# Gated linear attention on Trainium2: the loop written out, the group preparation half a beat earlier, both gates in one product, one PSUM bank of two per batch

## The chip, the core and the metric

The kernel runs on one core of one Trainium2 chip. It is one launch that computes a whole decoder of two layers in nine phases, one after the other. The metric is the device time of the launch in microseconds; of several runs the median counts. The change touches one phase, gated linear attention ("gla"), which takes some 580 us of the launch.

## The reference, cut to what matters

x is 64 batches of 128 tokens by 128 channels, in float32. The phase computes `x = layernorm(x + _L1_attn_ref(x, ...))` with 16 heads (H) of 8 channels (d):

```python
Q = (X @ q1_w.T).reshape(b, l, H, d)
K = (X @ k1_w.T).reshape(b, l, H, d)
V = X.reshape(b, l, H, d)
W = K[..., :, None] * V[..., None, :]
G = jax.nn.sigmoid(X.reshape(b, l, H, d) @ gw_w.T)
G = jnp.clip(G, 1e-06, None)
Gc = jnp.exp(jnp.clip(jnp.cumsum(jnp.log(G), axis=1), -30.0, 30.0)) + 1e-06
R = jax.nn.silu(K @ sw_w.T)[..., None]
Wc = jnp.cumsum(W * R / Gc[..., None], axis=1) * Gc[..., None]
O1 = jnp.einsum('blhd,blhde->blhe', Q, Wc)
E = V[:, 1:] - O1[:, :-1]
...
W2 = jnp.cumsum(K2[..., :, None] * E[..., None, :], axis=1)
O2 = jnp.einsum('blhd,blhde->blhe', Qm, W2)
out = (O1.reshape(b, l, dim) + O2.reshape(b, l, dim)) @ c_proj_w.T
```

Two gates come from the same rows: G from X and R from K = X @ k1_w.T. Qm is a leaky rectifier of the queries, K2 a sigmoid of a third projection.

## The kernel before, in words

Each cumulative sum is written as masked attention: scores of keys against queries, a triangular mask, a product with the values. A batch goes through three stages: s1 (four score products into the four banks `sc`, mask, into `a1`, then v1, sixteen products of 32 columns that give O1 in bank `o1b`), e (E = V minus shifted O1, two products, copied to `ep`), s2 (four score products into the same four banks, mask, into `a2`), v2 (O2 in bank `o2b`) and out (two products with `wo`). Of the four score banks VectorE masks two directly from PSUM (L2265 for s1, L2293 for s2). ScalarE copies the other two to SBUF (L2183, L2192), and GpSimd masks them there (L2332, L2342).

The work is pipelined over batches by hand. A **step** is a group of four batches, a **beat** (p = 0 to 3) one batch. In a beat TensorE does, in this order: s1 of batch n, e of batch n-2 (L2083, L2084), out of batch n-3 (L2089, L2090), a first half of the next group's preparation (`head(..., (p, 0))`), s2 of batch n-1, the second half (`(p, 1)`), v1 of n-1 and v2 of n-2 (L2063). ScalarE reads O1 and O2 out (L2200, L2206) at the end of its beat. The engines run their own instruction streams in order and meet at semaphores; there is no other scheduler.

The preparation of a group (`head`), per engine in order: GpSimd copies X to `xc`; TensorE transposes it (L2022) and ScalarE reads it as `xT`; the keys (L2028, read as `kT`); both gates, eight small products, four from `xT` with `gw` and four from `kT` with `sw` (L2032, L2033); VectorE takes them as `ga` and `gr` (L2224, L2225), ScalarE applies Exp, Ln, Exp (L2147 to L2151), VectorE finishes them (L2231, L2233); K2 (L2035, `k2a` on VectorE L2227, three ScalarE activations L2154 to L2158); the queries (L2038, `qT`, `qs`, L2235 `qmT`); the cumulative gate (L2041, clip L2239, Exp, L2242, reciprocal, L2246 `rg8`); both gates spread by transposition (L2046, L2051); and the products `kf` (L2250) and four `qg` (L2254), which the next group's s1 needs. ScalarE also writes four `qn` (L2172), which s2 needs. VectorE further does, once per group, the statistics of the four finished rows in beat 2 (L117, L121) and the normalisation in beat 3 (`normalise`, four instructions, L134); GpSimd computes the inverse deviation in between (L126, L128).

The first step, the last two steps and the first preparation stand outside the hardware loop; the 14 steps between run in a loop of two steps per turn (`run`, L1972 to L1980). What a batch needs first is asked for by the wait that names all of the group's VectorE instructions:

```python
if b == 0:
    pe.wait_ge(by_dve, (g + 1) * N_DVE)
```

## Time and profile before

| | us |
|---|---|
| runs shown, median of 3 | 3989.52 |
| lowest and highest | 3985.66, 3991.07 |
| profiled execution, device time | 3961.34 |
| its span | 3959.3 |
| the phase's first to last TensorE product | 2630.5 to 3194.7 |

In the profiled execution TensorE is busy 87% of the span, VectorE 64%, ScalarE and GpSimd 50% each; the granted clock of TensorE is 0.925 of full speed. In the profile a line number names the instruction's place in the code, `XC<-gla_scores` its output and input. An idle time in brackets is the time the engine stood still just before, with the instruction whose semaphore came last.

### The profile page before, as it was taken

Reading aid. Unit: us, or ns where it says so; the run is one execution under the profiler, and the core shown is the slowest. Engines: PE = TensorE matmul, PEld = TensorE weight load, DVE = VectorE, ACT = ScalarE, POOL = GpSimd, SP = SyncE. Lnnn points to the kernel's source line nnn. Section 1 sums busy time; section 2 is a strip of 40 time slices with the busy share of each in tenths; the row PEclk is TensorE's granted clock in tenths of the full one; section 3 lists DMA queues with packets and bytes.
Section 4 is the critical chain, followed back from the end, with each engine's and each line's share of the span. In section 5 each row is a group of like instructions: output and inputs, shape, how many; then the busy total and the mean of one; then the engine's idle time right before and its main releaser. Section 6 shows DMA issues by size and latency. Waiting matters only on the chain. (4 is left out here: it accounts for less than half of the span.)

```text
span 3959.3 us, 104241 instructions
## 1 busy us (share of the span) xinstructions
PE 3444.1 (87%) x41696; PEld 2239.8 (57%) x41696; DVE 2546.9 (64%) x5780; ACT 1967.4 (50%) x3810; POOL 1998.7 (50%) x1726
## 2 busy tenths in 40 slices
PE   7888988988599999886999998868888879999676
PEld 3444444544355555564666666645555557777676
DVE  6878878878477677475556647666666645554365
ACT  5555555554255555442665653335555536664254
POOL 5767667666377777654111115436666621111555
PEclk8999999999799999997999999979999979998598
DMA  3212121211920000000000000000000000000386
GB/s 123 76 71 78 69 80 70 77 72 62 297 65 2 2 2 2 16 1 17 5 5 5 5 3 10 5 6 2 2 2 2 2 11 6 7 6 12 99 266 197
DMA packets 48993, 182.11 MB, mean 46 GB/s; under 512 B 11679, under 2 KB 23074, under 8 KB 39361
## 3 DMA queue, kind: packets, MB, share of 16 engines
q1 hardware_dynamic: 44224, 167.68, 12.7%
q0 software_dynamic: 4352, 8.47, 0.6%
q8 instruction: 312, 5.11, 0.5%
q14 instruction: 105, 0.85, 0.1%
HBM read 167.13 MB, written 43.65 MB: 53 GB/s over the span
## 5 line engine op out<-in xcount | busy, mean ns | idle before, releaser
L494 DVE TENSOR_TENSOR_SCAN XC<-ssm_dA,ssm_db 128x2048 f32<-128x2048 f32 x128 | 565.6, 4419 | 145.0 <-PE ssm_db L349 122.0
L556 POOL TENSOR_TENSOR XC<-XC,XB 128x1536 f32<-128x1536 f32 x128 | 492.9, 3851 | 293.1 <-DVE XC L494 180.5
L363 PE MATMUL ssm_y<-XC,ssm_wt 128*128 128x512 f32 x1024 | 493.3, 626 | 1.6 <-POOL XC L556 1.6
L1130 POOL TENSOR_TENSOR self_pm<-self_pT,self_wt 128x512 f32<-128x512 f32 x256 | 321.9, 1292 | 175.6 <-ACT self_pT L904 175.6
L438 ACT ACTIVATE ssm_dA<-ssm_delta,ssm_nega 128x508 f32<-128x508 f32 x512 | 324.9, 707 | 106.2 <-DVE XC L494 106.2
L363 PEld LDWEIGHTS ssm_y<-XC,ssm_wt 128*128 128x128 f32 x1024 | 196.0, 199 | 228.7 <-issue 219.3
L1136 POOL TENSOR_TENSOR XC<-XC,XB 128x128 f32<-128x128 f32 x128 | 58.7, 459 | 402.3 <-DVE XB L1038 402.3
L2332 POOL TENSOR_TENSOR XC<-XC,gla_wt 128x512 f32<-128x512 f32 x128 | 160.6, 1275 | 157.7 <-ACT XC L2183 157.7
L349 PE MATMUL ssm_db<-XB,ssm_dxT 32*128 32x128 f32 x4096 | 174.6, 299 | 71.9 <-DVE XC L494 70.3
L349 PEld LDWEIGHTS ssm_db<-XB,ssm_dxT 32*128 32x128 f32 x4096 | 145.6, 198 | 136.7 <-DVE XC L494 113.0
L1457 DVE TENSOR_REDUCE narrow_nmax<-narrow_scores 128x4 f32<-128x308 f32 x256 | 105.1, 472 | 156.4 <-PE narrow_scores L1274 156.3
L904 ACT ACTIVATE self_pT<-self_scores 128x512 f32<-128x512 f32 x256 | 132.2, 602 | 137.2 <-PE self_scores L814 137.2
L126 POOL TENSOR_SCALAR narrow_rstd<-narrow_mv 128x4 f32<-128x4 f32 x16 | 3.6, 228 | 379.6 <-DVE narrow_mv L121 379.6
L1024 DVE TENSOR_REDUCE self_nmax<-self_scores 128x4 f32<-128x512 f32 x256 | 158.6, 680 | 46.8 <-PE self_scores L788 46.8
L2342 POOL TENSOR_TENSOR XC<-XC,gla_wt 128x512 f32<-128x512 f32 x128 | 160.9, 1278 | 42.9 <-ACT XC L2192 42.6
L1606 PEld LDWEIGHTS mlp_yp<-mlp_wt,mlp_h 128*128 128x128 f32 x1024 | 133.2, 192 | 58.1 <-issue 56.4
L904 ACT ACTIVATE cross_pT<-cross_scores 77x512 f32<-77x512 f32 x256 | 131.0, 591 | 69.8 <-PE cross_scores L814 69.6
L1382 ACT ACTIVATE narrow_pT<-narrow_scores 77x512 f32<-77x512 f32 x256 | 131.0, 591 | 68.4 <-PE narrow_scores L1300 68.4
L2265 DVE TENSOR_TENSOR XC<-gla_scores,gla_wt 128x512 f32<-128x512 f32 x128 | 82.4, 685 | 100.3 <-PE gla_scores L2057 100.3
L1634 ACT ACTIVATE mlp_h<-mlp_hp,mlp_bias 128x512 f32<-128x512 f32 x128 | 88.0, 687 | 109.0 <-PE mlp_hp L1598 109.0
L1024 DVE TENSOR_REDUCE cross_nmax<-cross_scores 128x4 f32<-128x308 f32 x256 | 104.0, 467 | 57.8 <-PE cross_scores L788 57.8
L1598 PE MATMUL mlp_hp<-mlp_zT,mlp_wt 128*128 128x512 f32 x256 | 134.3, 611 | 1.5 <-ACT mlp_zT L1628 1.5
(430 smaller groups left out, 8690.4 us busy)
## 6 DMA issues: line engine op xcount, KB each, us to landing
XB<-c_rows SPq DMA_DIRECT2D x64, 1024.0 KB, 4.7
experts_we<-in_w_experts SPq DMA_DIRECT2D x72, 579.0 KB, 4.6
sorted<-in_padding SPq DMA_DIRECT2D x1, 33280.0 KB, 112.2
experts_rt<-sorted SPq DMA_DIRECT2D x72, 65.0 KB
ssm_xT<-in_xT SPq DMA_DIRECT2D x16, 256.0 KB, 4.6
self_wt<-in_w_self SPq DMA_DIRECT2D x1, 1412.0 KB, 6.5
mlp_wt<-in_w_mlp SPq DMA_DIRECT2D x1, 1347.0 KB, 5.7
cross_ctx_t<-in_ctx SPq DMA_DIRECT2D x16, 77.0 KB
```

The lines of the kernel that those rows point to most:

```text
L349: mm = pe.matmul(of_batch(db, b)[:, :, 32 * c:32 * c + 32], dxT[rows, slot, half, c, :], diag(slot, c)[rows, nq, :].rearrange("p (k t) -> ...
L363: mm = pe.matmul(yp[half][:, :].rearrange("p (b t) -> p b t", b=GROUP), ident, of_state(states(32, at), k), start=False, stop=(nq == 3 and ...
L438: o = act.activation(dA[:, p % 2, :].rearrange("p (b k t) -> p b k t", b=GROUP, k=4)[:, :, k, 1:T], by_batch(delta[:, slot, half, :])[:, : ...
L494: dve.tensor_tensor_scan(states(0, p).rearrange("p m t -> p (m t)"), dA[:, p % 2, :], db[:, :], 0.0, ALU.mult, ALU.add).then_inc(h_ready, 1)
L556: pool.tensor_tensor(states(32, p).rearrange("p (b k) t -> p b k t", k=4)[:, :, 0:3, :], states(0, p).rearrange("p (b k) t -> p b k t", k= ...
L904: act.activation(pT[0:TK, n % 2, r, :], sc[r][0:TK, :], ACT.Exp).then_inc(exp_ready, 1)
L1024: dve.tensor_reduce(nmax[:, r, :], sc[r][:, 0:4 * TK].rearrange("p (h t) -> p h t", h=4), AX.X, ALU.max, negate=True).then_inc(max_ready, 1)
L1130: pool.tensor_tensor(pm[:, n % 2, r, :].rearrange("p (h t) -> p h t", h=4), pT[:, n % 2, r, :].rearrange("p (h t) -> p h t", h=4), bcast(V ...
L1598: pe.matmul(hp[j][:, :], w2[:, j * P:(j + 1) * P], zT[:, g % 2, :]).then_inc(h_mm, 1)
L1606: mm = pe.matmul(yp[g % 2][:, b * C:(b + 1) * C], h[:, g % 2, j, b * T:(b + 1) * T], w3[:, j * C:(j + 1) * C], start=(j == 0), stop=(j == 3))
L2332: pool.tensor_tensor(a1(b, r), a1(b, r), bcast(tri, 1, 4), ALU.mult).then_inc(m1_pool, 1)
L2342: pool.tensor_tensor(a2(b, r), a2(b, r), bcast(tri0, 1, 4), ALU.mult).then_inc(m2_pool, 1)
```

## The change

It does five things, all in this phase.

1. The hardware loop is gone: 17 steps are written out, with constant semaphore values and addresses.
2. The preparation is moved: transposes and `xT` in (0,0), keys and `kT` in (0,1), gates in (1,0), K2 and the gates' finish in (1,1), cumulative gate and queries in (2,0), `rg8`'s transposes, `kf` and `qmT` in (2,1), `gc8`'s transposes and the four `qg` in (3,0). On ScalarE the four `qn` move behind the read-outs of O1 and O2 in beats 2 and 3. On VectorE the normalisation moves from ahead of the read-out of `out` in beat 3 to the end of that beat.
3. Both gates are one product of `xT`: `gs` holds `gw` and `wkT @ sw` side by side (made once at the start), so four products of 32 columns take the place of eight of 16.
4. O1, e, out and O2 of a batch share one bank, `acc[b % 2]`, 128 columns each, in place of `o1b` and `o2b`. v1 of a batch waits for the read-out of the batch two before it (`out_read`); its waits for `o1_ready` and `e_ready`, and v2's for `out_read`, are gone.
5. GpSimd's copy of X to `xc` is gone: the transposes and `vp` read X.

```diff
-            step(0, 0, True)
-            with eng.Fori(1, NG - 2, 2) as g:
-                step(g, 1, True)
-                step(g + 1, 0, True)
-            step(NG - 1, 1, False)
-            step(NG, 0, False)
+            for g in range(NG + 1):
+                step(g, g % 2, g + 1 < NG)
...
+            pe.matmul(pj[1][:, 0:H], wkT, sw).then_inc(fold_mm, 1)
...
+                if half == (1, 0):
                     pe.wait_ge(by_act, g * N_ACT + 2)
                     for b in range(GROUP):
-                        pe.matmul(pj[1][:, b * H:(b + 1) * H], xT[:, b * T:(b + 1) * T], gw)
-                        mm = pe.matmul(pj[1][:, BH + b * H:BH + (b + 1) * H], kT[:, b * T:(b + 1) * T], sw)
+                        mm = pe.matmul(pj[1][:, b * 2 * H:(b + 1) * 2 * H], xT[:, b * T:(b + 1) * T], gs[:, :])
                     mm.then_inc(proj_mm, 1)
+                if half == (1, 1):
                     pe.matmul(pj[0][:, :], wk2, xT[:, :]).then_inc(proj_mm, 1)
                 if half == (2, 0):
-                    pe.wait_ge(by_dve, g * N_DVE + 3)
+                    pe.wait_ge(by_dve, g * N_DVE + 5)
+                    pe.matmul(pj[1][:, 2 * BH:3 * BH], tri, ga[:, 0, :]).then_inc(proj_mm, 1)
                     pe.matmul(pj[0][:, :], wq, xT[:, :]).then_inc(proj_mm, 1)
                 if half == (2, 1):
-                    pe.wait_ge(by_dve, g * N_DVE + 4)
-                    pe.matmul(pj[1][:, 2 * BH:3 * BH], tri, ga[:, 0, :]).then_inc(proj_mm, 1)
-                if half == (3, 0):
-                    pe.wait_ge(by_act, g * N_ACT + 10)
-                    pe.wait_ge(by_dve, g * N_DVE + 10)
+                    pe.wait_ge(by_act, g * N_ACT + 11)
+                    pe.wait_ge(by_dve, g * N_DVE + 9)
                     for b in range(GROUP):
                         mm = pe.matmul(pj[0][:, b * T:(b + 1) * T], rg8[:, b * P:(b + 1) * P], ident)
                     mm.then_inc(proj_mm, 1)
...
-                        if needed(n):
-                            pe.wait_ge(o1_ready, n)
                         if needed(n - 1):
-                            pe.wait_ge(e_ready, n - 1)
-                        if lagged(g, p, 2, slot):
-                            pe.wait_ge(e_ready, n)
-                        values(o1b, vp[:, s, b], a1, b, av1_mm)
+                            pe.wait_ge(out_read, n - 1)
+                        values(vp[:, s, b], a1, b, 0, av1_mm)
...
+            def shifted_queries(g, slot, p):
+                if p >= 2:
+                    act.wait_ge(by_dve, g * N_DVE + 11)
+                    for j in {2: (0, 1), 3: (2, 3)}[p]:
                         act.activation(by_batch(qn[:, slot, j, :])[:, :, 1:T], by_batch(qmT[:, :])[:, :, 0:T - 1],
                                        ACT.Identity, scale=own_head[:, j:j + 1]).then_inc(by_act, 1)
...
                 if half == (1, 1):
+                    dve.wait_ge(by_act, g * N_ACT + 5)
+                    dve.tensor_scalar(ga[:, 0, :], ga[:, 0, :], -1.0, float(np.log(1e-6)), ALU.mult, ALU.max)\
+                        .then_inc(by_dve, 1)
+                    dve.tensor_tensor(gr[:, 1, :], gr[:, 1, :], ga[:, 1, :], ALU.mult).then_inc(by_dve, 1)
                     dve.wait_ge(proj_mm, g * PJ + 4)
                     dve.tensor_scalar(k2a[:, :], pj[0][:, :], -0.02 / float(np.sqrt(C)), BIG, ALU.mult, ALU.min)\
                         .then_inc(by_dve, 1)
```

VectorE, beats 1 and 2 of a step, before. L2265 masks s1, L2293 masks s2; the gates' finish is L2231 and L2233.

```order
L2293 TENSOR_TENSOR XC<-gla_scores,gla_wt 128x512 x2
L2222 ISA
L2224 TENSOR_SCALAR gla_ga<-gla_proj 128x128
L2225 COPY gla_gr<-gla_proj 128x128
L2226 REGISTER_ALU
L2227 TENSOR_SCALAR gla_k2a<-gla_proj 128x512
L2261 REGISTER_ALU
L2265 TENSOR_TENSOR XC<-gla_scores,gla_wt 128x512 x2
L2272 COPY gla_ep<-gla_first 128x16x8
```

And in the change, from the first look at the gates to the next beat's mask of s1. L2295 masks s2, L2270 masks s1.

```order
L2229 TENSOR_SCALAR gla_ga<-gla_proj 128x128
L2230 COPY gla_gr<-gla_proj 128x128
L2295 TENSOR_TENSOR XC<-gla_scores,gla_wt 128x512 x2
L2233 TENSOR_SCALAR gla_ga<-gla_ga 128x64
L2235 TENSOR_TENSOR gla_gr<-gla_gr,gla_ga 128x64
L2237 TENSOR_SCALAR gla_k2a<-gla_proj 128x512
L2270 TENSOR_TENSOR XC<-gla_scores,gla_wt 128x512 x2
```

The gates' finish, which stood in beat 2 behind the statistics, now stands in beat 1 directly behind the mask of s2, and `k2a` stands behind it.

ScalarE, beats 1 and 2, before. L2192 copies s2's scores for GpSimd, L2200 and L2206 read out O1 and O2.

```order
L2192 ACTIVATE XC<-gla_scores 128x512 x2
L2146 ISA
L2147 ACTIVATE gla_ga<-gla_ga 128x128
L2148 ISA
L2149 ACTIVATE gla_ga<-gla_ga 128x128
L2150 REGISTER_ALU
L2151 ACTIVATE gla_ga<-gla_ga 128x64
L2200 ACTIVATE gla_o1T<-gla_first 128x128
L2206 ACTIVATE gla_o2T<-gla_second 128x128
```

And in the change. L2186 copies s2's scores, L2194 and L2200 read out O1 and O2.

```order
L2139 ACTIVATE gla_ga<-gla_ga 128x128
L2141 ACTIVATE gla_ga<-gla_ga 128x128
L2143 ACTIVATE gla_ga<-gla_ga 128x64
L2186 ACTIVATE XC<-gla_scores 128x512 x2
L2146 ACTIVATE gla_k2a<-gla_k2a 128x512
L2148 ACTIVATE gla_k2a<-gla_k2a 128x512
L2150 ACTIVATE gla_k2T<-gla_k2a 128x512
L2194 ACTIVATE gla_o1T<-gla_out 128x128
L2200 ACTIVATE gla_o2T<-gla_out 128x128
```

The gates' three functions now stand ahead of s2's copy, and the three of K2, which followed in beat 2, now stand between that copy and the read-out of O1.

## Rows read from the trace of the kernel before

**Rows 1.** Timeline of TensorE: start us, busy us, line, operation, [idle before, releaser]; s1 at a step's start
```profile
2753.11 1.14 PE L2057 MATMUL gla_scores<-gla_qg,gla_kf 32*128 32x512 f32 x8 [3.02 <-DVE gla_qg L2254]
...
3162.23 1.14 PE L2057 MATMUL gla_scores<-gla_qg,gla_kf 32*128 32x512 f32 x8 [2.53 <-DVE gla_qg L2254]
```

**Rows 2.** Waits, 2670 to 3140 us: waiter, releaser, us in all, times, longest
```profile
PE gla_scores L2057 <- DVE gla_qg L2254: 38.6, 14, 3.2
...
PE gla_first L2083 <- ACT gla_o1T L2200: 9.2, 14, 0.7
...
PE gla_scores L2057 <- DVE XC L2293: 4.6, 14, 1.1
...
PE gla_proj L2041 <- DVE gla_ga L2231: 4.4, 13, 0.3
```

**Rows 3.** Timeline of TensorE in one group
```profile
2800.13 0.38 PE L2033 MATMUL gla_proj<-gla_wt,gla_kT 128*128 128x16 f32 x2
2800.36 1.10 PE L2035 MATMUL gla_proj<-gla_xT,gla_wt 128*128 128x512 f32 x2
...
2803.28 1.14 PE L2057 MATMUL gla_scores<-gla_qg,gla_kf 32*128 32x512 f32 x8
2804.35 0.49 PE L2083 MATMUL gla_first<-gla_neg,gla_o1T 128*128 128x128 f32 x2
...
2805.34 1.02 PE L2038 MATMUL gla_proj<-gla_xT,gla_wt 128*128 128x512 f32 x2
...
2807.77 0.43 PE L2041 MATMUL gla_proj<-gla_ga,gla_wt 128*128 128x64 f32 x2 [0.34 <-DVE gla_ga L2231]
...
2821.59 1.14 PE L2057 MATMUL gla_scores<-gla_qg,gla_kf 32*128 32x512 f32 x8 [3.20 <-DVE gla_qg L2254]
```

**Rows 4.** Windows: from:to, us, busy (count) of PE, PEld, DVE, ACT, POOL, granted clock, DMA
```profile
2822.90:2826.30 3.40, 3.40 (x16) 1.92 (x15) 1.76 (x4) 1.06 (x2) 2.49 (x2) 0.51 0.02 5
3162.20:3166.20 4.00, 3.65 (x36) 1.94 (x40) 1.90 (x5) 1.30 (x3) 2.09 (x2) 1.00 0.00 0
```

**Rows 5.** Timeline, 2668 to 2670 us: GpSimd's masks beside VectorE's gate operations
```profile
2668.07 1.09 ACT L2183 ACTIVATE XC<-gla_scores 128x512 f32<-128x512 f32 x2 [0.79 <-PE gla_scores L2057]
2668.75 2.51 POOL L2332 TENSOR_TENSOR XC<-XC,gla_wt 128x512 f32<-128x512 f32 x2 [1.86 <-ACT XC L2183]
...
2669.48 0.60 DVE L2231 TENSOR_SCALAR gla_ga<-gla_ga 128x64 f32<-128x64 f32 x1
...
2670.00 1.35 DVE L2233 TENSOR_TENSOR gla_gr<-gla_gr,gla_ga 128x64 f32<-128x64 f32 x1
```

**Rows 6.** Source line 2242: ns min/median/max, first and last start; then the tail's normalisation
```profile
L2242 DVE TENSOR_SCALAR gla_gc<-gla_gc x16: 195/929/944, 2645.8 to 3152.1; 128x64 f32<-128x64 f32 x16
...
3181.47 4.00 DVE L134 TENSOR_SCALAR X<-gla_y,gla_mv,gla_rstd 128x128 f32<-128x128 f32 x4
```

**Rows 7.** Timeline of VectorE in the same group
```profile
2800.75 0.28 DVE L2225 COPY gla_gr<-gla_proj 128x128 f32<-128x128 f32 x1
...
2804.49 1.29 DVE L2265 TENSOR_TENSOR XC<-gla_scores,gla_wt 128x512 f32<-128x512 f32 x2 [2.29 <-PE gla_scores L2057]
...
2806.20 0.88 DVE L117 BATCH_NORM_STATS2 gla_stats<-gla_y 128x6 f32<-128x128 f32 x4
2807.24 0.38 DVE L121 BATCH_NORM_AGGREGATE gla_mv<-gla_stats 128x2 f32<-128x6 f32 x4 [0.16 <-DVE gla_stats L117]
...
2810.23 0.22 DVE L2239 TENSOR_SCALAR gla_gc<-gla_proj 128x64 f32<-128x64 f32 x1
...
2812.33 0.69 DVE L2246 TENSOR_TENSOR gla_rg<-gla_rg,gla_gr 128x512 f32<-128x512 f32 x1
...
2818.16 2.71 DVE L2254 SCALAR_TENSOR_TENSOR gla_qg<-gla_qT,gla_wt,gla_proj 128x512 f32<-128x512 f32 x4
```

**Rows 8.** Timeline of ScalarE in the same group
```profile
2801.75 0.26 ACT L2151 ACTIVATE gla_ga<-gla_ga 128x64 f32<-128x64 f32 x1
...
2805.46 0.63 ACT L2154 ACTIVATE gla_k2a<-gla_k2a 128x512 f32<-128x512 f32 x1
```

More of the change, by code:

```diff
@@ L1957, in linear_attention_phase @@
         sc = [ph.bank(f"scores{r}") for r in range(4)]
-        o1b = ph.bank("first")
-        o2b = ph.bank("second")
+        acc = [ph.bank(f"out{i}") for i in range(2)]
         pj = [ph.bank(f"proj{i}") for i in range(2)]
-        (loaded, power_set, setup, zeroed, xc_ready, vp_ready, proj_mm, by_act, by_dve, s1_mm, s2_mm, m1_dve, m1_act,
+        (loaded, power_set, setup, zeroed, fold_mm, folded, vp_ready, proj_mm, by_act, by_dve, s1_mm, s2_mm, m1_dve, m1_act,
          m1_pool, m2_dve, m2_act, m2_pool, av1_mm, o1_ready, e_mm, e_ready, av2_mm, o2_ready, out_mm, out_read, vec,
          pool_step, x_out) = (ph.sem(n) for n in (
-             "loaded", "power_set", "setup", "zeroed", "xc_ready", "vp_ready", "proj_mm", "by_act", "by_dve", "s1_mm",
+             "loaded", "power_set", "setup", "zeroed", "fold_mm", "folded", "vp_ready", "proj_mm", "by_act", "by_dve", "s1_mm",
              "s2_mm", "m1_dve", "m1_act", "m1_pool", "m2_dve", "m2_act", "m2_pool", "av1_mm", "o1_ready", "e_mm",
@@ L1989, in closing @@
         def closing(g):
-            return not (isinstance(g, int) and g < 1)
+            return g >= 1
         def a1(b, r):
@@ L2024, in head @@
-                if half == (1, 0):
+                if half == (0, 0):
+                    if g:
+                        pe.wait_ge(by_dve, (g - 1) * N_DVE + 10)
+                    for b in range(GROUP):
+                        mm = pe.transpose(pj[0][:, b * T:(b + 1) * T], X[:, g * GROUP + b, :], ident)
+                    mm.then_inc(proj_mm, 1)
+                if half == (0, 1):
                     pe.wait_ge(by_act, g * N_ACT + 1)
-                    if needed(g):
+                    pe.wait_ge(folded, 2)
+                    if g:
@@ L2082, in step @@
                         pe.wait_ge(o1_ready, n + 1)
-                        pe.matmul(o1b[:, T:T + C], o1T[:, b % 2, :], neg[:, :], start=True, stop=False)
-                        pe.matmul(o1b[:, T:T + C].rearrange("p (r j d) -> p r j d", r=4, j=4), up, spread(vp[:, s, b]),
+                        e = acc[b % 2][:, T:T + C]
+                        pe.matmul(e, o1T[:, b % 2, :], neg[:, :], start=True, stop=False)
+                        pe.matmul(e.rearrange("p (r j d) -> p r j d", r=4, j=4), up, spread(vp[:, s, b]),
                                   start=False, stop=True).then_inc(e_mm, 1)
@@ L2124, in step @@
                         pe.wait_ge(m2_pool, 2 * (n + 1))
-                        if needed(n):
-                            pe.wait_ge(out_read, n)
-                        values(o2b, ep[:, b % 2], a2, b, av2_mm)
-            run(pe, head, step)
+                        values(ep[:, b % 2], a2, b, 3 * T, av2_mm)
+            run(head, step)
         @block.scalar
@@ L2205, in step @@
                             act.wait_ge(out_mm, n)
-                        act.activation(o2T[:, :], o2b[:, 0:T], ACT.Identity).then_inc(o2_ready, 1)
-            run(act, head, step)
+                        act.activation(o2T[:, :], acc[b % 2][:, 3 * T:4 * T], ACT.Identity).then_inc(o2_ready, 1)
+                    if more:
+                        shifted_queries(g + 1, 1 - slot, p)
+            for half in HALVES:
+                head(0, 0, half)
+            for p in range(GROUP):
+                shifted_queries(0, 0, p)
+            for g in range(NG + 1):
+                step(g, g % 2, g + 1 < NG)
         @block.vector
@@ L2296, in step @@
                         head(g + 1, 1 - slot, (p, 1))
-            run(dve, head, step)
+                    if p == 3 and closing(g):
+                        dve.wait_ge(pool_step, g * 2)
+                        normalise(dve, lambda b: X[:, (g - 1) * GROUP + b, :], lambda b: y[:, 1 - slot, b, :],
+                                  mv[:, :, :], rstd[:, :]).then_inc(x_out, 1)
+            run(head, step)
         @block.gpsimd
@@ L2343, in step @@
                                                ALU.mult).then_inc(m2_pool, 1)
-            run(pool, head, step)
+            run(head, step)
 def experts_phase(nc, env, name, wd, w, out):
```

120 lines of the change are left out of this document (50 added, 70 removed).

## The prediction

> **What bounds the kernel now.** I read the timeline of TensorE first. Two starts of s1 at a step's start lie 409.12 us and twelve steps apart [rows 1], so a step of four batches takes 34.09 us. The chain of waits then says where TensorE stands still in 14 steps: 38.6 us behind the four `qg`, 9.2 behind the read-out of O1, 4.6 behind the masks of s2, 4.4 behind the gates [rows 2]. That is 56.8, or 4.06 us a step, and 2.76 of it is one stop: s1 of a new group waits for the last `qg`. A second loss follows it. After the stop TensorE runs 3.4 us at a granted clock of 0.51, its 1.2 GHz level, though it is busy throughout [rows 4], which costs half of that, 1.7 us. The other stops of 2.7 us and more are followed by such a fall too; the one of 2.53 us [rows 1] is followed by a full clock [rows 4]. So a step is 34.09 = 4.06 idle + 1.7 slow + 28.3 of products at full clock. TensorE is the bound, broken by VectorE's chain.
>
> The reader should also see what VectorE's small operations cost. In rows 5, GpSimd's two masks run from 2668.75 to 2671.26; VectorE's finish of the first gate, 64 columns, takes 0.60 us, until GpSimd's first mask is over, and that of the second takes 1.35 us, until the second is over. The addition to `gc` takes 195 ns with GpSimd idle and 929 ns as a rule [rows 6]. And the last normalisation, four small instructions, takes 4.00 us [rows 6]. An SBUF-to-SBUF instruction of VectorE waits for the GpSimd instruction that runs, and gets one chance between two of them. The Trainium skill (SBUF — State Buffer, "Who interferes with whom") has this as an exclusive lock on a shared port pair, in which the order of issue decides who blocks; the rows above agree.
>
> **Part by part, gates first.** A gate product's place is 0.23 us (2800.13 to 2800.36) [rows 3]; four of eight go, so 0.9 us a step. The keys' part is folded into the weights once, for one product and two copies: nothing. The copy of X on GpSimd was off the path, and so is its absence. The banks: v1 now waits for the sum `y` of the same beat, which VectorE does right after its masks and `ep`, while TensorE has e, out, half a preparation and s2 to do: nothing, and that is some 3 us of cover. The loop: its turn shows no stop of its own in the waits; I take nothing.
>
> **The stop on `qg` goes.** The spread of `gc8` moves a half ahead, the four `qg` stand before the mask of s2 in beat 3, and the normalisation behind it. What is late next is that mask. Count from s1 of beat 3: s1 and e, out end at 1.07 + 0.99 = 2.06 [rows 3]. Four `gc8` products, as long as e and out with their loads, end near 3.2. Four `qg` take 2.7 [rows 7], to 6.0, and the mask 1.29 [rows 7], to 7.3. TensorE has s2 (1.07) and v1 and v2 (1.9) after the `gc8` products and is done at 6.1. **Stop C: 1.2 us**, in place of 2.76.
>
> **The order of beat 1 decides the rest.** Count from the end of the gate products. VectorE takes its second copy 0.39 later, ScalarE its third function 1.00 after that [rows 3, 7, 8], s2's copy some 0.2 later, and GpSimd's first mask 0.68 after that copy starts [rows 5]: 2.26. VectorE must mask s2 first: s2 1.07, hand-over 0.14, masks 1.20 to the next instruction: 2.41, and only then comes the gates' finish. So GpSimd starts first, by 0.15 us. The finish of the first gate then waits for one mask of 1.25, that of the second for the next, and is done at 2.26 + 2.5 + 0.1 = 4.86 instead of about 2.6. `k2a` follows until 5.5. Beat 2 starts at 1.07 + 2.92 (K2, v1, v2, 2800.36 to 2803.28) = 3.99. So `k2a` ends 1.5 into beat 2. ScalarE's three functions of K2, 0.63 each [rows 8], end at 3.4, and **only behind them** comes the read-out of O1, which e waits for, 0.3 more: 3.7. TensorE has been free since 1.07. **Stop A: 2.6 us**, where rows 2 have 0.66.
>
> **Beat 2.** e and out end at 4.65, the sum `y` at 5.3. The statistics take 1.33 (2806.20 to past 2807.53) [rows 7], then the chain from clip to `rg8`, 2810.23 to 2813.02 = 2.79 [rows 7]. In it `gc`'s addition now meets GpSimd only in its small operations, so 0.74 less: 2.05. That is 8.7. Meanwhile TensorE does tri (0.4), queries (1.0) and s2 (1.07), ready at 7.05, and in the new order waits for `rg8` there. **Stop B: 1.7 us.** The old waits of 0.34 for the gates, 0.33 for the masks of s2 and 0.66 for O1 go.
>
> **The sum.** A step was 34.09. Out go 4.06 idle, 1.7 slow, 0.9 gates; in come A + B + C = 5.5, less 0.2, as these count from the end of issue and rows 2 from the end of work: 5.3. That is 32.7 us. Its price is between 0 (all under B) and 1.7 (all outside); I take 0.5, nearer to the cover. Step: 33.2, or 0.9 less. Over 15 steps: 13.5 us. The **first preparation** is a bare chain at the low clock: four gate products less at twice 0.23 is 1.8; GpSimd's copy ahead of the transposes, between 0 and a mask's 1.25, say 0.6; the gate's Exp no more behind two activations like those of rows 8, 1.2; in all 4 (bounds 2 and 5). In the **tail** the sum `y` stood behind the 4.00 us of rows 6 and v2 behind it: 2 (bounds 0 and 3). Together 19.5 us: the profiled execution's 3961.3 would become 3941.8. That execution is 28.2 below the median of the runs; on the median it is 3989.5 - 19.5 = **3970 us**.
>
> **A rule against it and one for it.** The Trainium skill (TensorE: Matmul & The Clock Gate, "Why this matters for your kernels") names a length of gap below which the clock keeps up, and 2.6 lies below it; by it the falls would be gone and the result 7 us lower. Its section on oscillation there tells of a kernel that fell once for each short tile, which is the first rival.
>
> **Rivals.**
> 1. *Every fall at full price.* For: stops A, B and C make three chances a step, and a fall that begins late lies on v1 and v2, with no slack. Against: B's slack follows A directly. Step 32.7 + 1.7 = 34.4; 15 x 0.3 = 4.5 lost, 6 won at the ends: 3988. Chance 0.17.
> 2. *VectorE wins the race of beat 1.* The margin is 0.15 us in 2.3. Then the gates finish at 2.6, `k2a` ends ahead of beat 2, O1 is read at 1.7 into it, A shrinks to 0.6; `rg8` comes earlier too, at 7.5, but s2 ends at 5.2, so B is 2.3; C is 1.1 and M1 behind the normalisation adds 0.3. Idle 4.3, step 31.7 without falls, 32.6 with them in half of the steps: 15 x 1.5 to 2.4 and 6: 28 to 42 lower, 3954 in the middle. Chance 0.23.
> 3. *Slower: the normalisation meets GpSimd.* It now runs behind the mask of s2 in beat 3, beside GpSimd's masks of the same scores. I expect one wait, as its last mask is just ending. If GpSimd lags by more than one mask, each of the four waits, 4.00 us as in rows 6, and the next s1's mask, due 1.3 us after the normalisation's free run, comes some 2.4 late, s2 with it. It decides from the point where GpSimd's next pair starts before the second of the four. Step 33.2 + 2.4 = 35.6: 15 x 1.5 = 23 lost, 6 won: 4007. Chance 0.1.
> 4. *The written-out streams stall on code*, or the change does not do what it says: no row of this phase shows it, the phases around it are written out and TensorE runs full there. Chance 0.05, for either sign.
>
> My forecast has 0.45.
>
> **How the numbers follow.** About 0.2%, 8 us, is what a measurement of this kernel can tell from no change. Faster takes the forecast (0.45), rival 2 (0.23) and a little of the fourth: 0.7. Same is rival 1: 0.18. Slower is rival 3 and the rest: 0.12. The forecast's own range is 3960 to 3982 (fall 0 to 1.2 a step, ends 2 to 8). The range leaves out the far half of rival 2 and rival 3: 3946 to 3994.
>
> **What would show it.** In the profile after: no wait of s1 on `qg`; a wait of e (the product with `neg`) on the read-out of O1 of about 2.6 us once a step; a wait of the `rg` transposes on `rg8` of about 1.7; s1 on the mask of s2 about 1.2; the second gate's product on VectorE near 1.3 us instead of 0.21, and `gc`'s addition near 0.2; four gate products a step. Steps of 33.2 us. It is wrong if the second gate stays at 0.21 (rival 2), if the normalisation takes 4 us (rival 3), or if TensorE stands still for another reason than these three.

## The result, and the profile after

| | before | after |
|---|---|---|
| median (lowest to highest), us | 3989.35 (3979.49 to 3991.07), 5 runs | 3952.53 (3938.21 to 3967.42), 5 runs |
| ratio to before, 95% interval | | 0.9917 [0.9898, 0.9935] |
| profiled execution: time, span | 3961.34, 3959.3 | 3938.21, 3936.4 |
| gla, in the profiled execution | 582.1 | 541.8 |
| narrow attention, the phase behind it | 434.7 | 428.6 |
| experts, the last phase | 324.2 | 346.8 |

The change is faster by 36.8 us on the medians; the interval of the ratio means 26 to 41 us. The forecast was 19.5 us. The profiled execution of the kernel before is none of its five runs and lies 18 us below their lowest. Phases are measured between the starts of the weight transfers that open them.

The first thing to see is that the phase that was edited gained 40.3 us, while the profiled pair differs by 23.1. The rest lies in phases that the change does not touch: narrow attention is 6.1 us shorter, and the experts are 22.6 us longer. The experts show ScalarE standing still without a releaser, six times, once for 13.70 us. Timeline of ScalarE, then the waits of 3580 to 3940 us, after:

```profile
3685.60 0.21 ACT L2540 ACTIVATE experts_alpha<-experts_best 128x4 f32<-128x4 f32 x1 [13.70 <-issue]
```
```profile
ACT experts_alpha L2540 <- issue: 27.6, 6, 13.7
```

The same kernel run again on another chip had 325.1 us there, and so had every experiment, within 2 us. So the change does not bring it. Whether it belongs to this one execution or to the chip of this measurement stays open: on that chip the medians of both kernels, 3989 and 3953 us, lie 27 and 22 us above those of the same kernels in the experiments, 3962 and 3930. A reader who had compared the two spans alone would have halved the gain of the edit.

**TensorE's waits after**, 2670 to 3120 us (waiter, releaser, us in all, times, longest), beside [rows 2]:

```profile
PE gla_out L2081 <- ACT gla_o1T L2194: 24.4, 14, 2.4
PE gla_proj L2043 <- DVE gla_rg L2248: 22.2, 14, 1.7
PE gla_scores L2054 <- issue: 15.4, 14, 1.1
```

The 38.6 us on `qg` are gone, and the waits on the masks and the gates too. What is left are the three stops that the prediction called A (e on the read-out of O1), B (`rg8`'s transposes) and C (s1 behind the mask of s2). On the timeline of TensorE they look like this:

```profile
2727.30 0.49 PE L2081 MATMUL gla_out<-gla_neg,gla_o1T 128*128 128x128 f32 x2 [2.40 <-ACT gla_o1T L2194]
...
2732.31 1.13 PE L2043 MATMUL gla_proj<-gla_wt,gla_rg 128*128 128x128 f32 x8 [1.69 <-DVE gla_rg L2248]
...
2758.43 0.49 PE L2081 MATMUL gla_out<-gla_neg,gla_o1T 128*128 128x128 f32 x2 [1.26 <-ACT gla_o1T L2194]
...
2763.43 1.59 PE L2043 MATMUL gla_proj<-gla_wt,gla_rg 128*128 128x128 f32 x8 [1.69 <-DVE gla_rg L2248]
2764.95 1.94 PE L2060 MATMUL gla_out<-XC,gla_vp 128*32 128x128 f32 x32
...
2775.16 1.14 PE L2054 MATMUL gla_scores<-gla_qg,gla_kf 32*128 32x512 f32 x8 [1.11 <-issue]
```

Stop A has two lengths, 2.40 us in six steps (one of them 2.38) and 1.26 in eight. Stop C names no releaser, but VectorE's timeline does: the mask of s2 (two instructions, 1.28 us from 2773.78) ends as s1 starts, and the normalisation behind it runs free, four instructions in 1.31 us:

```profile
2773.78 1.28 DVE L2295 TENSOR_TENSOR XC<-gla_scores,gla_wt 128x512 f32<-128x512 f32 x2
2774.97 1.31 DVE L134 TENSOR_SCALAR X<-gla_y,gla_mv,gla_rstd 128x128 f32<-128x128 f32 x4
```

Added up, the idle time did not fall. It is (24.4 + 22.2 + 15.4) / 14 = 4.43 us a step, against 4.06 before. What fell is the time at the low clock, and the work between the stops. Windows of TensorE after (from:to, us, busy (count) of PE, PEld, DVE, ACT, POOL, granted clock): behind a stop of 2.40 us the clock stays full in five of six steps; the falls lie at 2764, 2825 and 2893, and there are no others.

```profile
2728.30:2731.30 3.00, 2.32 (x14) 0.73 (x12) 2.31 (x13) 1.03 (x4) 2.92 (x4) 1.00 0.00 0
2764.00:2767.40 3.40, 3.40 (x53) 3.00 (x56) 1.77 (x3) 0.48 (x2) 1.79 (x2) 0.51 0.02 5
2825.50:2828.90 3.40, 3.40 (x14) 1.45 (x13) 2.50 (x14) 1.24 (x4) 3.19 (x4) 0.52 0.01 2
```

In the kernel before, 13 of the same fourteen steps had a fall, the first of them 6.8 us long. Only the step that began behind a stop of 1.27 us had none.

**Where a step's time went.** Over the fourteen steps behind the first, a step took 34.11 us before and 31.85 after, 2.26 less. Windows over these steps, before and then after, and of single steps in two of the experiments below. In `e4` (the kernel before, written out) they are a step with a fall and one without, in `e6` (the change with eight gate products) one without:

```profile
2684.70:3162.23 477.53, 418.39 (x5545) 266.55 (x5545) 314.13 (x714) 256.86 (x560) 313.53 (x279) 0.95 0.01 2
2679.05:3124.97 445.92, 383.79 (x5433) 245.97 (x5433) 321.47 (x711) 255.77 (x561) 307.19 (x267) 0.99 0.01 2
```
```profile
2811.74:2845.44 33.70, 29.90 (x396) 19.30 (x396) 22.45 (x51) 18.37 (x40) 22.43 (x20) 0.95 0.01 2
2879.15:2911.68 32.53, 28.42 (x397) 18.29 (x397) 22.35 (x51) 18.38 (x40) 22.45 (x20) 1.00 0.01 2
```
```profile
2818.06:2850.05 31.99, 27.94 (x397) 18.22 (x397) 22.58 (x52) 18.24 (x41) 21.99 (x20) 1.00 0.01 2
```

With the short gaps that the waits leave out, TensorE's idle time rose from 4.22 to 4.44 us a step, and its busy time fell by 2.47, from 29.89 to 27.41. Of this, 1.1 us are the falls: one makes a step's products 1.5 us longer before (29.90 against 28.42) and 1.6 after, in fourteen steps fourteen times (the long one counted twice) against three. The gate products are 0.9. The last 0.5 us are products that take less time in the new order: `e4` and `e6` both have eight gate products and no loop, and they have 28.42 and 27.94 us of work in a step at full clock. The hardware loop has no part in it, as its cost lies in the idle time (see `e4`). Outside these steps, the first step gained 2.1 us, its start 4.4 (3.5 of it behind the first product), and the tail 2.2: there v1 waits 0.84 us for the sum `y`, where v2 waited 2.26 before.

**The race of beat 1.** VectorE's two operations that finish the gates meet GpSimd's two masks of s2. Source lines, ns min/median/max:

```profile
L2233 DVE TENSOR_SCALAR gla_ga<-gla_ga x16: 195/1060/1067, 2639.0 to 3104.7; 128x64 f32<-128x64 f32 x16
```
```profile
L2235 DVE TENSOR_TENSOR gla_gr<-gla_gr,gla_ga x16: 211/213/1343, 2639.1 to 3105.7; 128x64 f32<-128x64 f32 x16
```
```profile
L2244 DVE TENSOR_SCALAR gla_gc<-gla_gc x16: 195/195/339, 2642.2 to 3113.2; 128x64 f32<-128x64 f32 x16
```

The first waits as forecast, 1.06 us, and `gc`'s addition is free at 0.195 where it took 0.929 [rows 6]. The second has two outcomes. First a step with A = 2.40, then one with A = 1.26, timelines of GpSimd and VectorE:

```profile
2721.89 2.53 POOL L2340 TENSOR_TENSOR XC<-XC,gla_wt 128x512 f32<-128x512 f32 x2 [0.73 <-ACT XC L2186]
```
```profile
2723.15 1.34 DVE L2235 TENSOR_TENSOR gla_gr<-gla_gr,gla_ga 128x64 f32<-128x64 f32 x1
```
```profile
2754.15 2.61 POOL L2340 TENSOR_TENSOR XC<-XC,gla_wt 128x512 f32<-128x512 f32 x2 [0.72 <-ACT XC L2186]
```
```profile
2754.43 1.06 DVE L2233 TENSOR_SCALAR gla_ga<-gla_ga 128x64 f32<-128x64 f32 x1
2755.41 0.21 DVE L2235 TENSOR_TENSOR gla_gr<-gla_gr,gla_ga 128x64 f32<-128x64 f32 x1
```

In the first, VectorE gets one operation in between the two masks and stands behind the second mask with the other, until 2724.4. In the second it gets both in, and GpSimd's pair takes 0.08 us longer. The 1.13 us saved pass straight through `k2a`, K2's three functions and the read-out of O1: A is 1.14 us shorter, and so is the step (31.12 against 32.26 us).

### The profile page after: what moved, and what is told of

The parts are those of the page before. It is cut to its first block and busy times, and to the rows that moved or that the text cites. A ratio compares the mean times of both kernels' runs of the same rounds, so it can differ in the third digit from the quotient of the medians.

```text
span 3936.4 us, 102778 instructions
## 1 busy us (share of the span) xinstructions
PE 3398.2 (86%) x41570; PEld 2210.2 (56%) x41570; DVE 2549.1 (65%) x5782; ACT 1967.2 (50%) x3810; POOL 1991.1 (51%) x1710
## 5 line engine op out<-in xcount | busy, mean ns | idle before, releaser
L2270 DVE TENSOR_TENSOR XC<-gla_scores,gla_wt 128x512 f32<-128x512 f32 x128 | 82.4, 686 | 80.5 <-PE gla_scores L2054 79.4
```

## The experiments

Each ratio is to the kernel before on the same chip. There its medians were 3962.94 us (runs `e1` to `e4`), 3961.95 (`e5` to `e8`) and 3960.49 (`e9`, `e10`); times of one chip are compared with each other. The first three runs attack stop A, the largest.

### e1: the read-out of O1 ahead of K2's functions

```diff
                 if half == (1, 1):
-                    act.wait_ge(by_dve, g * N_DVE + 5)
-                    act.activation(k2a[:, :], k2a[:, :], ACT.Exp).then_inc(by_act, 1)
...
                         act.activation(o2T[:, :], acc[b % 2][:, 3 * T:4 * T], ACT.Identity).then_inc(o2_ready, 1)
                     if more:
+                        third_keys(g + 1, 1 - slot, p)
```

`third_keys` holds the wait and the three functions, and runs in beat 1.

> The changed kernel with one thing moved on ScalarE: K2's three functions stand behind the read-outs of O1 and O2 in beat 1, not ahead of them. Theory (ScalarE's order makes stop A: e waits for O1, which is queued behind K2's functions, which wait for VectorE behind GpSimd's masks): the waits of 2.40 and 1.26 us of e on the read-out of O1 are gone; the copies of s1 come later instead, up to 1 us is given back before s2; steps of 31.1 and 32.3 us become 30.2, some 24 us less than the change in the phase. Rival (the chain from the sum y to rg8 carries beat 2 whatever O1 does): stop B grows by what A loses, steps stay within 0.3 us of 31.1, and the time stays.

Measured: 3907.37 us, ratio 0.9865 [0.9844, 0.9885]; phase 530.2, steps of 30.77 but for one of 32.38 with a fall and one of 30.54. Waits of TensorE, same stretch:

```profile
PE gla_proj L2043 <- DVE gla_rg L2254: 23.2, 15, 2.3
PE gla_scores L2054 <- issue: 16.6, 15, 1.1
PE gla_scores L2054 <- ACT XC L2180: 14.4, 13, 1.1
```

Stop A is gone. It was the order on ScalarE, then, and not the computation of O1. Of A's 1.26 to 2.40 us, 1.1 came back as a wait of s2 for ScalarE's copy of scores, which now queues behind K2's functions. The step is still 0.35 us shorter than the change's short one and 1.5 shorter than its long one, and all falls but one are gone.

### e2: the gates' finish ahead of the mask of s2

```diff
-                if half == (1, 1):
                     dve.wait_ge(by_act, g * N_ACT + 5)
                     dve.tensor_scalar(ga[:, 0, :], ga[:, 0, :], -1.0, float(np.log(1e-6)), ALU.mult, ALU.max)\
                         .then_inc(by_dve, 1)
                     dve.tensor_tensor(gr[:, 1, :], gr[:, 1, :], ga[:, 1, :], ALU.mult).then_inc(by_dve, 1)
+                if half == (1, 1):
                     dve.wait_ge(proj_mm, g * PJ + 4)
```

The two operations fall to half (1, 0), which VectorE does ahead of its mask of s2.

> The changed kernel with the gates' finish on VectorE ahead of the mask of s2 in beat 1, so that it runs before GpSimd's masks of the same scores begin. Theory (the finish waits for the GpSimd instruction that runs, then for the next): the finish of the first gate falls from 1.06 us to 0.2, that of the second from 1.34 or 0.21 to 0.21 in every step, e's wait for O1 to 0.6 us, steps to 30.5 to 31.1 us, and steps of 32.3 are gone: 10 to 20 us less than the change. Rival (the small instructions are slow by themselves, or wait for ScalarE): they stay near 1 us and the time stays or rises by 5 us, since the mask of s2 is now behind a wait for ScalarE.

Measured: 3910.13 us, ratio 0.9865 [0.9845, 0.9885]; phase 528.0, steps of 30.64 but for one of 32.24 with a fall. The two operations take 0.196 and 0.219 us in every step: ahead of the mask there is no GpSimd to meet. Waits:

```profile
PE gla_proj L2043 <- DVE gla_rg L2248: 24.5, 15, 1.7
PE gla_scores L2054 <- issue: 16.6, 15, 1.1
PE gla_out L2081 <- ACT gla_o1T L2194: 11.8, 15, 0.9
```

So the race, taken out, is worth as much as the last link of the chain to O1: A is 0.8 us here, in every step. `e1` and `e2` are 56 and 53 us below before, where the change run again (`e5`) is 31.5 below.

### e3: both

The edits of `e1` and `e2` together.

> Both moves of the two runs before. Theory: no stop A, stop B 1.8 us, stop C 1.1 us, steps of 30.1 us, no fall of the clock between the first step and the last; 25 to 30 us less than the change. Rival (beat 2 is carried by VectorE's chain): no better than the better of the two alone.

Measured: 3915.07 us, ratio 0.9884 [0.9864, 0.9904]; phase 531.1.

```profile
PE gla_proj L2043 <- DVE gla_rg L2254: 33.8, 15, 2.3
PE gla_scores L2054 <- issue: 16.6, 15, 1.1
```

Together they are no better than either. Part of that is the clock: the profiled execution had three falls, one of 6.8 us, in steps of 31.88, 33.45 and 32.14 us, and the other eleven steps took 30.54. That alone is 0.1 to 0.2 us less than in `e1` and `e2`, and the waits say why it is no more. No wait on O1 is left, but the wait on `rg8` has grown from 1.6 to 2.3 us. TensorE and VectorE in one beat 2, which starts with s1 at 2789.75:

```profile
2796.58 1.13 PE L2043 MATMUL gla_proj<-gla_wt,gla_rg 128*128 128x128 f32 x8 [2.31 <-DVE gla_rg L2254]
```
```profile
2792.36 0.28 DVE L2289 TENSOR_TENSOR gla_y<-gla_out,X 128x128 f32<-128x128 f32 x1
2792.68 0.87 DVE L117 BATCH_NORM_STATS2 gla_stats<-gla_y 128x6 f32<-128x128 f32 x4
2793.70 0.38 DVE L121 BATCH_NORM_AGGREGATE gla_mv<-gla_stats 128x2 f32<-128x6 f32 x4
...
2794.51 0.62 DVE L2250 TENSOR_SCALAR gla_gc<-gla_gc 128x64 f32<-128x64 f32 x1 [0.32 <-ACT gla_gc L2146]
```

The same places measured in four kernels, in us. The first column counts from the start of s1 of beat 2 to the sum `y`, the second is the addition to `gc`, the third counts from `y` to the transposes of `rg8`, the last from s1 to them:

| | s1 to `y` | addition | `y` to transposes | s1 to transposes |
|---|---|---|---|---|
| `e2` | 3.12 | 0.20 | 3.81 | 6.93 |
| `e3` | 2.61 | 0.62 | 4.22 | 6.83 |
| `e8` (below) | 3.11 | 1.28 | 3.49 | 6.60 |
| `e10` (below) | 2.61 | 0.73 | 3.39 | 6.00 |

TensorE has e 0.8 us earlier in `e3`, and the sum `y` comes 0.5 earlier, as VectorE is busy with its mask of s1 until then. Of these 0.5 the addition takes 0.42 back: it now starts while GpSimd still has its mask. So 0.1 us is left, and the step shows it (30.54 against 30.64). The chain to `rg8` sets the end, and 1.3 us of it are the statistics. Runs `e8` and `e10` go on from there.

### e4: the kernel before, written out

```diff
-            with eng.Fori(1, NG - 2, 2) as g:
-                step(g, 1, True)
-                step(g + 1, 0, True)
+            for g in range(NG + 1):
+                step(g, g % 2, g + 1 < NG)
```

> The kernel before with the loop written out and nothing else. Theory (the loop's registers and turn cost little): 2 us less in the phase, 0.25 us for each second step, with all the stops and falls of before; 0 to 5 us less in all. Rival (the written-out code is what brings or takes time): more than 10 us less in the phase, or stalls without a releaser in this or the later phases and 10 us or more above before.

Measured: 3954.47 us, ratio 0.9982 [0.9972, 0.9991], 4 to 11 us; phase 570.5 against 582.1. Most steps are 33.7 us instead of 34.1, and four are 32.53. Both are more than was expected: the phase is 11.6 us shorter in the profiled execution, and 10.2 of it lie in the fourteen steps.

```profile
PE gla_scores L2053 <- DVE gla_qg L2250: 34.0, 14, 2.5
PE gla_first L2079 <- ACT gla_o1T L2196: 9.2, 14, 0.7
```

The stop on `qg` is 2.4 us a step instead of 2.76, the other waits are as before. VectorE is not what became faster: in both kernels its last `qg` ends 10.5 us behind the start of s1 of beat 3. But TensorE starts the next s1 0.25 us after that end between the two steps of a turn and 0.5 to 0.7 us after it where a turn ends (at 2821.59 0.72 us: the `qg` of [rows 7] end at 2820.87), and 0.05 us after it in `e4`. The loop thus cost 0.3 to 0.4 us a step on TensorE's own side, and it showed as part of the wait on `qg`. The four short steps are those without a fall, and one of them began behind a short stop of 1.07 us. Of the 13 stops of 2.53 us, three had no fall behind them, while before each stop of 2.73 us and more had one.

### e5 and e6: the change again, and with eight gate products

`e5` is the change as it stands. The edit of `e6`:

```diff
-                        mm = pe.matmul(pj[1][:, b * 2 * H:(b + 1) * 2 * H], xT[:, b * T:(b + 1) * T], gs[:, :])
+                        pe.matmul(pj[1][:, b * 2 * H:b * 2 * H + H], xT[:, b * T:(b + 1) * T], gw)
+                        mm = pe.matmul(pj[1][:, b * 2 * H + H:(b + 1) * 2 * H], kT[:, b * T:(b + 1) * T], sw)
```

> The changed kernel once more, unaltered. Its first profile lost 22.6 us in the last phase (experts, 346.8 us against 324.2 before), in which nothing is changed, in stops of up to 13.7 us without a releaser. Theory (these belong to single executions or places, not to the change): the experts phase takes 324 to 326 us as in the three kernels derived from it, gla 541 to 545 us, and the kernel stands 40 to 47 us below the one before. Rival (the change brings them): experts again near 347 us and some 25 to 33 us below.

> The changed kernel with the gates as eight products of 16 columns again (the folded weights are made but not used). Theory (four products more are 0.9 us a step on TensorE, on the path): steps 0.9 us longer, the first preparation 1.8 us, 15 us in the phase. Rival (the later gates are hidden, as beat 1 has no stop of TensorE): a change within 3 us, or the race between VectorE's finish and GpSimd's first mask comes out another way and steps differ by 1.1 us either way.

Measured: `e5` 3930.45 us, ratio 0.9912 [0.9893, 0.993], phase 550.8, experts 325.1; `e6` 3943.56, ratio 0.9943 [0.9929, 0.9957], phase 565.1. Steps without a fall are 31.12 in the one and 32.0 in the other: 0.9 us, the four places of 0.23 us in [rows 3], and 13.1 us on the time. The waits are alike (rg 18.6 and 18.0, O1 27.2 and 26.2 us), so it is work and not a stop that goes. Of the expectation for `e5`, the experts came true; its phase and its distance from the kernel before did not, and the falls are the larger part of why.

`e5` also shows the same program with eight falls in the fourteen steps, where the other execution had three, with steps of up to 33.85 us and a phase 9 us longer. The stops are the same (2.4 or 1.25, 1.69, 1.1), with the long A in seven steps. The falls cost 10.0 us over the fourteen steps, against 3.4; `e6` and `e9` had eight as well. On TensorE's timeline a fall is seen in the durations: e takes 0.80 us instead of 0.49, the transposes 1.83 instead of 1.13. The window shows that the fall at 2764 was a long one:

```profile
2764.52 0.80 PE L2081 MATMUL gla_out<-gla_neg,gla_o1T 128*128 128x128 f32 x2 [2.39 <-ACT gla_o1T L2194]
...
2931.03 1.83 PE L2043 MATMUL gla_proj<-gla_wt,gla_rg 128*128 128x128 f32 x8 [1.69 <-DVE gla_rg L2248]
```
```profile
2764.00:2770.80 6.80, 6.28 (x21) 3.27 (x21) 3.38 (x14) 2.95 (x8) 3.77 (x4) 0.50 0.00 1
```

The fall at 2764 began in the last half microsecond of A and lasted 6.8 us, twice as long as the others; stop B is gone in that step, and still it is 33.50 us, 1.24 longer than one without a fall. A fall of 3.4 us behind the same stop, at 2733, cost nothing, and one at 2798 cost 0.8. The one at 2931 began behind B and cost 1.6.

### e7: the normalisation back ahead of the read-out of `out`

```diff
+                    if p == 3 and closing(g):
+                        dve.wait_ge(pool_step, g * 2)
+                        normalise(dve, lambda b: X[:, (g - 1) * GROUP + b, :], lambda b: y[:, 1 - slot, b, :],
+                                  mv[:, :, :], rstd[:, :]).then_inc(x_out, 1)
...
                         dve.tensor_tensor(y[:, s, b, :], acc[b % 2][:, 2 * T:2 * T + C], X[:, n, :], ALU.add).then_inc(out_read, 1)
...
-                    if p == 3 and closing(g):
-                        dve.wait_ge(pool_step, g * 2)
-                        normalise(dve, lambda b: X[:, (g - 1) * GROUP + b, :], lambda b: y[:, 1 - slot, b, :],
```

> The changed kernel with the normalisation back where it was, ahead of the read-out of out in beat 3 on VectorE. Theory (VectorE's chain in beat 3 sets stop C: the sum y, the qg and the mask of s2 all come 1.4 to 2 us later, and v1, which now waits for the sum, too): stop C grows from 1.1 to 2.4 to 3 us, steps by 1.3 to 1.9 us, 20 to 28 us in the phase, with more falls of the clock. Rival (no difference, as the normalisation must be done anyway before the next mask): within 3 us.

Measured: 3993.00 us, ratio 1.0067 [1.0052, 1.0082]; phase 609.2, 58 us longer than `e5`. One move turns the change from 31.5 us faster into 31 slower. VectorE, GpSimd and TensorE in one beat 3:

```profile
2900.06 3.67 DVE L134 TENSOR_SCALAR X<-gla_y,gla_mv,gla_rstd 128x128 f32<-128x128 f32 x4
2903.65 0.28 DVE L2287 TENSOR_TENSOR gla_y<-gla_out,X 128x128 f32<-128x128 f32 x1
```
```profile
2899.65 2.49 POOL L2330 TENSOR_TENSOR XC<-XC,gla_wt 128x512 f32<-128x512 f32 x2 [4.38 <-ACT XC L2177]
```
```profile
2904.07 1.08 PE L2060 MATMUL gla_out<-XC,gla_vp 128*32 128x128 f32 x32 [2.43 <-DVE gla_y L2287]
```

Four small instructions meet GpSimd's masks of s1 and take 3.67 us where they take 1.31 behind the mask of s2. The sum `y` waits behind them, and v1 waits for `y` because O1 and out share a bank now. A step without a fall is 34.34 us against 31.12: 2.43 are this wait of v1, and 0.7 a longer stop C, where the expectation had put the growth. Over fourteen steps that is 45 of the 58 us. There were 15 falls in them, against eight in `e5`. This is the mechanism of rival 3, at a place which the change avoids. It also tells what parts 2 and 4 of the change owe each other: by the waits in the code, the shared bank is free of cost only because the normalisation was moved away. The move back with two banks was not run.

### e8: the statistics in beat 0 of the next step, on top of e2

```diff
-        y = ph.sb("y", [P, 2, GROUP, C])
+        y = ph.sb("y", [P, 3, GROUP, C])
...
-                    if p == 2 and closing(g):
-                        dve.wait_ge(out_read, g * GROUP)
-                        row_stats(dve, lambda b: y[:, 1 - slot, b, :], stats[:, :, :], mv[:, :, :], vec, (g - 1) * VEC, mark)
...
+                    if p == 0 and g >= 2:
+                        rows_of(g - 2)
+                    if p == 3 and g >= 2:
+                        norm_of(g - 2)
```

`rows_of` does the statistics of a group, at the end of beat 0; `norm_of` normalises it, a step later than before, and GpSimd's inverse deviation moves with it.

> The kernel with the early gate finish, and with the statistics of a group's rows moved out of beat 2 to the end of beat 0 of the next step (three slots of y, normalisation one step later). Theory (stop B is y, statistics, clip, Exp, addition, reciprocal, rg8, with 1.33 us of it the statistics): rg8 comes 1.3 us earlier if nothing else holds it, or 0.6 us if the addition or rg8 now meets GpSimd's masks, which it did not before; stop B from 1.6 to 0.3 or 1.0 us, steps of 29.4 to 30.1 us against 30.64, 8 to 19 us less than with the early finish alone. Rival (another chain takes over): steps of 30.6 us again.

Measured: 3900.96 us, ratio 0.9842 [0.9828, 0.9855]; all fourteen steps 30.31 to 30.33 us, no fall. The wait on `rg8` fell only from 1.6 to 1.3 us (20.1 us in 15), though 1.3 us of statistics left the path to it. The source line of the addition shows where the rest went:

```profile
L2244 DVE TENSOR_SCALAR gla_gc<-gla_gc x16: 195/1286/1298, 2643.1 to 3093.0; 128x64 f32<-128x64 f32 x16
```

Starting earlier, the chain runs into GpSimd's masks of s1, which it used to miss: 1.29 us instead of 0.20, 1.1 of the 1.3 given back. It is the wait of beat 1 again, met by a chain that had become faster.

### e9: two banks again

```diff
-        acc = [ph.bank(f"out{i}") for i in range(2)]
+        o1b = ph.bank("first")
+        o2b = ph.bank("second")
...
+                            pe.wait_ge(o1_ready, n)
...
-                            pe.wait_ge(out_read, n - 1)
+                            pe.wait_ge(e_ready, n - 1)
+                        if lagged(g, p, 2, slot):
+                            pe.wait_ge(e_ready, n)
...
+                            pe.wait_ge(out_read, n)
```

> The change with O1 and O2 in two banks again and the old waits (v1 on the read-outs of O1 and of the same batch's e, v2 on the read-out of out). My theory: none of these waits is the last one anywhere, neither before nor after, so the three stops stay at 2.4 or 1.3, 1.7 and 1.1 us and the step within 0.3 us of the change's 31.1 to 32.7: a phase of 535 to 555 us, the time within 5 us of the change run beside it earlier (3930 by the scatter of its falls of the clock). Rival: the one bank is what lets TensorE go on to v1 in beat 1, whose e comes late behind the read-out of O1; then the waits of v1 on e_ready show with over 0.3 us a step, a phase over 560 us and a time near 3945.

Measured: 3927.92 us, ratio 0.9919 [0.9902, 0.9937] beside 0.9912 in `e5`; phase 552.8 beside 550.8. The same three waits (28.9, 15.6 and 15.5 us), none of v1 or v2. The theory held: the banks are worth nothing here by themselves.

### e10: e8 and e1

The edits of `e8` (with that of `e2` in it) and of `e1` together.

> The version with the statistics apart and the gates' finish early (3901), and besides ScalarE's three functions of K2 behind the read-outs of O1 and O2. It takes out its last wait for O1, 0.8 us a step. My theory: stop B is set by VectorE's chain to rg8, which now meets GpSimd's masks (the addition takes 1.28 us until they are over), and what TensorE wins ahead of it is idled in front of rg8, as with both reorderings at once (3915 against 3907 and 3910). Steps of 30.2 to 30.5, the wait for rg8 near 2.2 us, time 3898 to 3910. Rival: the chain starts from tri, which TensorE issues earlier by the 0.8, so it finishes earlier too, and the step falls to 29.6: a phase of 512 us and 3890.

Measured: 3896.33 us (3887.86 to 3898.66), ratio 0.9837 [0.982, 0.9854]; phase 514.0, fifteen steps of 29.72 to 29.74, no fall behind the first of them. The expectation missed; its rival came true in the step. Waits, and VectorE in one beat 2:

```profile
PE gla_proj L2043 <- DVE gla_rg L2254: 20.9, 14, 1.5
PE gla_scores L2054 <- issue: 16.6, 15, 1.1
```
```profile
2781.42 0.28 DVE L2289 TENSOR_TENSOR gla_y<-gla_out,X 128x128 f32<-128x128 f32 x1
2781.62 0.21 DVE L2247 TENSOR_SCALAR gla_gc<-gla_proj 128x64 f32<-128x64 f32 x1
2782.22 0.73 DVE L2250 TENSOR_SCALAR gla_gc<-gla_gc 128x64 f32<-128x64 f32 x1 [0.38 <-ACT gla_gc L2146]
```

The table under `e3` explains the miss. In `e3` the sum `y` came 0.5 us earlier and the addition lost 0.42 to GpSimd by it. In `e8` the addition waits for GpSimd's mask in any case, so here the same 0.5 is kept: the chain starts earlier, meets the mask at another moment (0.73 in place of 1.28; the product `rg8` takes 1.10 in place of 0.69), and the transposes come 0.6 earlier, as does the next step. On the time alone `e8` and `e10` cannot be told apart, as their intervals overlap; on the step, 30.32 against 29.73, they can. It is the fastest version tried, 64 us below before on its chip's medians.

## Why the prediction was right, and where it was off

- **The stop on `qg` and its fall: right in kind.** The wait is gone, and stop C is 1.1 us where the count gave 1.2. The fall before was charged 1.7 us a step; it makes the products 1.5 us longer, and a step with one is 1.2 us longer than one without (`e4`: 33.70 and 32.53).
- **"Falls of the clock: A, at 2.6 ... so I expect most steps to have one."** It did not hold in the profiled execution, with three falls in fourteen steps, and did in `e5`, with eight. Falls followed a stop A of 2.4 us directly in one of six steps, and in `e5` in three of seven; the others came behind B, two and five. The price depends on where the fall begins. At 2825 the fall lay on the cumulative gate, the queries and s2, and stop B shrank from 1.69 to 0.24: that step is 32.44 us beside 32.26 without, so 0.2. At 2764 and 2893 it began behind stop B, on the transposes, v1 and v2, with nothing to absorb it: 32.72 and 32.73 beside 31.12, so 1.6. This is nearly the price that rival 1 took for every fall; that place for a fall it named rightly. Measured in all, 3.4 us over fourteen steps and 10.0 in `e5`, or 0.24 and 0.7 a step: the 0.5 taken lies between.
- **"The order of beat 1 decides the rest."** GpSimd starts first, as counted, and the first finish of a gate waits for one mask: 1.06 us. "That of the second for the next" is the step that failed: it did in six of fourteen steps only, and in `e5` in seven. Rival 2 had VectorE win before the first mask; what it did was win in the middle, between the two. A averages 1.74 us instead of 2.6, and this is the largest term of the miss: with B at 1.59 and C at 1.1 the three stops are 4.43 where the sum had 5.3.
- **Stop B: right.** 1.69 where 1.7 was counted. It is the same behind either length of A, since y, the statistics and TensorE's tri and queries all start from e and out.
- **The loop: its price was wrong, the sum was not hurt by it.** "I take nothing", because its turn showed no stop of its own. `e4` gives 0.3 to 0.4 us a step, inside the wait on `qg`, and that wait the sum takes out whole.
- **The products: a small term that the sum lacks.** It left 27.4 us of products for a step, and 27.2 were measured: the reordered ones take less time, which nothing in the prediction priced.
- **Gates, banks, ends: right.** 0.9 us a step (`e6`), nothing for the banks (`e9`), a first preparation of 3.5 for 4 and a tail of 2.2 for 2.

Against the forecast step of 33.2 the measured one is 1.35 us shorter: 0.87 of the stops, 0.26 of the falls, 0.22 of the products. Over fifteen steps that is the difference between 19.5 us and the phase's gain of 40. The medians show 36.8, and 31.5 when run again on another chip, where the profiled execution had five falls more. The measured 3952.5 us lies 17 below the forecast, outside the forecast's own 3960 to 3982 and inside the range only by the part of rival 2 that it takes in. That it came out at rival 2's 3954 is half its mechanism and half an accident: the rival had A at 0.6 and B at 2.3, measured are 1.74 and 1.59, and only the sums are close.

**A rule and the rows.** The falls at 2764 and 2893 follow a stop of 1.69 us with one of 1.26 us some 5 us ahead of it, and five of the six stops of 2.40 us are followed by none. The Trainium skill (TensorE: Matmul & The Clock Gate, "Why this matters for your kernels") names a single gap longer than all of these as what drops the clock; by it the fourteen steps would have had no fall in either execution of the change. They had three and eight, so gaps below it can be followed by a fall. At its price of nothing the rule is as far from the 0.24 us a step of the profiled execution as the forecast's 0.5 is, and further from the 0.7 of `e5`.

## What to carry to other kernels

Count a stop together with the fall of the clock behind it: here the waits of a step rose from 4.06 to 4.43 us, and the step shrank by 2.26; 1.1 of it came from falls, as several stops of up to 2.4 us were followed by fewer of them than one of 2.7 or more in each step. Ahead of a small SBUF-to-SBUF chain on VectorE, look up what GpSimd does at that moment in the new order; moving it a microsecond either way changed single instructions from 0.2 to 1.3 us (`e2`, `e8`) and four of them by 2.4 us with the whole gain of the change (`e7`). And when a wait is removed, follow the next chain operation by operation in the new timing: the same half microsecond was eaten by one addition in `e3` and kept in `e10`.

## What the runs showed of the hardware that was not expected

- Between two back-to-back GpSimd masks of 1.25 us, VectorE gets in one or two SBUF-to-SBUF operations of 64 columns (1.34 or 0.21 us for the second), and the same program shows both, in six and eight of fourteen steps, and in `e5` in seven and seven. The Trainium skill (SBUF — State Buffer, "Who interferes with whom") has it that whichever issues first holds the shared ports for its whole instruction; the waits agree. Who came first in the middle was not the same from step to step, though in both executions GpSimd began its masks 11.71 us and VectorE its two operations 11.99 us into every step, and what decides it stays open.
- The number of falls of the clock is not a property of the program: 3 and 8 in fourteen steps of two executions of the same one. In `e8` and `e10`, with no stop beyond 1.5 us, there were none in these steps. That is no safe limit: in `e1` one began at 2701.7, behind stops of 1.11 and 1.49 us. Nor do the falls explain the whole spread of the times: the runs of `e8` and `e10` lie within 9 and 11 us, those of `e1` to `e3`, with one to three falls, within 7, and those of `e5` within 23.
- The hardware loop cost time that no stop of its own shows: 0.25 us between the two steps of a turn and 0.5 to 0.7 us at its end, from VectorE's last `qg` to TensorE's next product, against 0.05 us written out.
- ScalarE stood still for 13.70 us without a releaser, in one of twelve profiled executions. Its cause is not known.

What stays open besides: the rearranged preparation was never run inside the hardware loop, so that the loop's 0.3 to 0.4 us are shown for the order before alone; GpSimd's copy (part 5) and the moves of the preparation other than that of the normalisation were not undone one by one, so their share is read from waits and not from a run; and why a stop of 2.4 us is followed by a fall at one time and not at another.
